# A fused alignment, attention and expert-mix kernel: the expert tiles placed two steps sooner, in the step that turns the last batch

## The reference, cut to what matters

```python
def reference(x, itok_BS_0_21, ...):
    h = _L0_tok_ref(x, itok_BS_0_21, ...)             # soft alignment, its gradient: [32, 128, 128]
    h = h + _L0_attn_ref(_layernorm(h), Wq, Wk, Wv, Wm)
    h = h + _L0_ffn_ref(_layernorm(h), Wg, W, V, W2)
    return h

def _L0_attn_ref(input1, Wq, Wk, Wv, Wm):
    ...
    A = -(Q[:, :, :, None] - K[:, :, None, :]) ** 2
    P = jax.nn.softmax(A / d ** 0.5, axis=-1)
    O = jnp.einsum('bhts,bhse->bhte', P, V)
    head_result = O.transpose(0, 2, 1, 3).reshape(B, T, E)
    return head_result @ Wm + input1

def _L0_ffn_ref(x, Wg, W, V, W2):
    topv, topi = jax.lax.top_k(jnp.einsum('bsd,de->bse', x, Wg), 2)
    ...
    for e in range(8):
        h = silu(x @ W[e]) * (x @ V[e])
        y = y + gw[..., e:e + 1] * (h @ W2[e])
```

## Time and profile before

| what | value |
|---|---|
| median of 3 runs | 694.59 us (694.49 to 696.78) |
| profiled execution, whole | 695.72 us |
| its span | 693.9 us |
| mean granted TensorE clock, share of full | 0.938 |
| PE busy | 370.7 us (53% of the span) |
| DVE busy | 496.9 us (72%) |
| ACT busy | 373.2 us (54%) |
| POOL busy | 228.7 us (33%) |

### The profile page before, as it was taken

One profiled execution on the slowest core, in us unless ns is written; L12 is line 12 of the kernel. 1 busy time (PEld: TensorE's weight loads), 2 busy tenths in 40 slices (PEclk: granted clock), 3 DMA queues, 4 the chain that ended last, 5 costly groups with the idle time before them and its releaser, 6 DMA issues.

```text
span 693.9 us, 13468 instructions
## 1 busy us (share of the span) xinstructions
PE 370.7 (53%) x3107; PEld 305.2 (44%) x3108; DVE 496.9 (72%) x1773; ACT 373.2 (54%) x1106; POOL 228.7 (33%) x430
## 2 busy tenths in 40 slices
PE   0400000000000127777767887789999999999930
PEld 0200000000000015555655665678888888888830
DVE  1969999999994578888988977876744444444425
ACT  0434444444442129998977989554455455544510
POOL 1035454545453000000004332465675333333320
PEclk9999999999999998988889979999999999999975
DMA  5177804040324332333250000122332111111129
GB/s 105 45 177 172 178 9 96 4 92 7 88 57 95 106 120 63 108 98 86 74 159 32 23 24 20 53 59 60 81 95 65 41 45 42 45 43 45 39 82 283
DMA packets 113096, 54.06 MB, mean 78 GB/s; under 512 B 56988, under 2 KB 108828, under 8 KB 112947
## 3 DMA queue, kind: packets, MB, share of 16 engines
q1 hardware_dynamic: 106478, 44.53, 26.4%
q0 software_dynamic: 4320, 8.47, 3.7%
q10 hardware_dynamic: 2237, 0.38, 0.4%
HBM read 29.61 MB, written 24.19 MB: 78 GB/s over the span
## 4 chain that ended last, share of the span: by engine, by line
DVE 34%; PE 34%; ACT 13%; issue 8%; DMA 7%; SPq 3%; ACTq 0%; DVEq 0%; POOLq 0%
PE ps L752 9%; PE ps L569 5%; DVE D L1196 5%; DVE D L1205 5%; PE ps L571 5%; PE ps L570 5%; PE ps L742 4%; DVE ps L1185 3%; ACT ps L851 3%; ACT D L857 3%; ACT sq L942 3%; DMA gb<-g_dram 3%; DVE mn L1365 2%; ACT sq L935 2%; DMA iota_sb<-in_iota 2%
## 5 line engine op out<-in xcount | busy, mean ns | idle before, releaser
L1087 POOL DMA_INDIRECT xd_dram<-pay,slot x64 | 62.2, 972 | 212.6 <-DVE pay L1444 185.4
L1108 POOL DMA_INDIRECT y_dram<-ybuf,dest x71 | 69.8, 983 | 100.1 <-DVE ybuf L1550 85.1
L1528 DVE TENSOR_TENSOR sq<-sq,ps 128x512 f32<-128x512 f32 x71 | 48.8, 688 | 70.1 <-PE ps L571 54.6
L605 PE MATMUL ps<-zdiag,ones_f 32*128 32x32 f32 x2 | 0.6, 408 | 181.3 <-DVE zdiag L1273 181.3
L1064 POOL TENSOR_TENSOR D<-D 128x128 f32<-128x128 f32 x130 | 56.2, 432 | 119.2 <-DVE D L1219 59.6
L990 ACT ACTIVATE sq<-ps 128x512 f32<-128x512 f32 x71 | 42.5, 598 | 75.7 <-PE ps L571 75.7
L857 ACT ACTIVATE D<-D 64x2 f32<-64x2 f32 (+1 forms) x154 | 31.3, 204 | 94.6 <-DVE D L1205 78.5
L605 PEld LDWEIGHTS ps<-zdiag,ones_f 32*128 32x128 f32 x2 | 0.5, 308 | 181.4 <-DVE zdiag L1273 181.4
L942 ACT ACTIVATE sq<-sq,mn 128x128 f32<-128x128 f32 x256 | 78.2, 397 | 0.0
L752 PE MATMUL ps<-wdn,xnt 128*128 x568 | 76.2, 277 | 1.9 <-issue 1.2
L752 PEld LDWEIGHTS ps<-wdn,xnt 128*128 128x128 f32 x568 | 69.0, 192 | 4.7 <-issue 4.7
(11 more groups left out here) (222 smaller groups left out, 1062.3 us busy)
## 6 DMA issues: line engine op xcount, KB each, us to landing
stage<-xd_dram SPq DMA_DIRECT2D x71, 65.0 KB
D<-th_dram SPq DMA_DIRECT2D x16, 208.0 KB, 4.0
g_dram<-D SPq DMA_DIRECT2D x14, 208.0 KB, 4.2
x_dram<-D SPq DMA_DIRECT2D x14, 208.0 KB, 4.4
h0q<-g_dram SPq DMA_DIRECT2D x8, 256.0 KB, 3.0
gb<-g_dram SPq DMA_DIRECT2D x8, 256.0 KB, 3.6
xf<-x_dram SPq DMA_DIRECT2D x8, 256.0 KB, 3.2
xb<-x_dram SPq DMA_DIRECT2D x8, 256.0 KB, 3.9
```

The costliest lines, as they stand in the source:

```text
L1087: pool.indirect_dma_start(xd_dram, bass.IndirectOffsetOnAxis(slot[:, q, j, k:k + 1], 0), pay[q % 3][:, k, j, :], None).then_inc(s_sc[2 * k ...
L1108: pool.indirect_dma_start(y_dram, bass.IndirectOffsetOnAxis(dest[:, w:w + 1], 0), yrow[w], None, bounds_check=2 * NB * T - 1, oob_is_err=F ...
```

## The change

START goes from NB + 1 to NB - 1, so tile k stands in step 31 + k. The first column and its copies move from the end of the step before the first tile to the tile's own step; on PE they stand ahead of `up(0)`. Since banks 5 and 6 are in use in step 31, `column(0)` waits for the copies of batch 31's turned scores. The wait for the copied head results (`s_num`) moves from `experts_begin` to the first `down`, since only bank 7 needs it. Nothing else is edited. The steps of the attention's pieces, of the sends, of the tables and of the first scatter keep their numbers. Because the condition in `root_second` contains START, quad 6 meets it too.

```diff
-        START, UNROLLED = NB + 1, 28
+        START, UNROLLED = NB - 1, 28
...
             def column(k, c):
 
+                if isinstance(k, int) and k < 1:
+                    pe.wait_ge(s_pta, pta(NB))
+                    pe.wait_ge(s_ptd, ptd(NB))
                 pe.wait_ge(s_xr[c], round_of(k, c))
...
             def down(k, c, e):
 
                 pe.wait_ge(s_ht, k + 1)
-                if not (isinstance(k, int) and k < 1):
+                if isinstance(k, int) and k < 1:
+                    pe.wait_ge(s_num, 2 * NQ)
+                else:
                     pe.wait_ge(s_y, k)
...
                 pe.wait_ge(s_sq, NB)
-                pe.wait_ge(s_num, 2 * NQ)
...
                 k = n - START
+                if k == 0:
+                    experts_begin()
+                    column(0, 0)
                 if k >= 0:
                     expert[k] = expert_of(k)
                     up(k, k % 4, expert[k])
...
-                if n == START - 1:
-                    experts_begin()
-                    column(0, 0)
```

More of the change, by code:

```diff
@@ L1021, in _ @@
                     weights_high(n + 1)
-                if n == START - 1:
+                k = n - START
+                if k == 0:
                     columns(0, 0)
-                k = n - START
                 if 0 <= k < UNROLLED:
```

## The result

The changed kernel takes 706.11 us (median of 6 runs, 704.14 to 709.57); the kernel before, on the same chip, takes 694.54 us (6 runs, 693.31 to 696.78). The ratio is 1.0168, with an interval of 1.0149 to 1.0187: slower by some 11.6 us. The forecast was 701.5 us, in a range of 696.7 to 705.8, and slower as the likeliest sign. So the sign came true, and the time is 0.3 us above the range and 4.6 us above the forecast. The 0.3 us are within the scatter of the runs: run again, the kernel took 10.1 us more than the one before.

A forecast was written before the change was run, and what follows sets the result against it. PE was taken to bound the tiles' stage. Start 1.3, table loads 2.8, first scatter 1.2 and clock 1.6 sum to 6.9 us over 694.6: 701.5 us, own range 698.3 to 704.9, stated range 696.7 to 705.8.

The forecast's parts named there:

- clock at the start: Half clock on PE behind the idle times at the first column and in step 32: 1.6 us together, bounds 0 and 3.2.
- What bounds the kernel: PE bounds the tiles' stage; the first tile's rows land at 447.67 wherever PE's order puts the column.
- The rival in which tiles fill the attention's waits: Rows present when PE asks, so tile work fills idle time: 690.4 us at best, chance 0.05.
- The first column: On PE at the first tile: waits 3.12 us for rows, 0.89 for copies, 0.10 ahead of `up(1)`; net 1.3 us more.
- The table loads: Two more ACT table loads in step 32 leave PE idle 2.8 us ahead of the third `up`, bounds 1.57 and 3.8.
- The rival with the page's price: ACT's table switch also pays the skill page's drain, 2.8 us dearer: 704.3 us, chance 0.04.
- The first scatter: At tile 16 DVE waits 2.9 us for scatter 0; 1.7 covered, PE idles 1.2 us, bounds 0 and 2.9.
- the clock stays down: Rival: tiles don't begin sooner and low clock lasts at the first tile, some 4 us more: 705.5 us, chance 0.16.
- From 500 us on nothing gives it back: From 500 us to the end no lost time returns, since PE stays the bound.
- the waits cover each other: Rival: start costs 1.3 us, table pair only 1.0, clock and scatter nothing: 696.9 us, chance 0.17.
- the far sum: All terms at far bounds: start 1.3, table loads 3.8, scatter 2.0, clock 3.2, together 10.3 us.
- the near sum: All terms at nearer bounds: start 1.3, table loads 1.6, scatter 0, clock 0.8, together 3.7 us.

The follow-up runs named there:

- rows of fewer quads: Changed kernel with the first table made from three quads instead of four (17 early tiles, all pads behind load 16): 704.68 us, ratio 1.0147 to the kernel before.
- the edit without the switch: Changed kernel with a plain copy for the silu of tiles 0 and 1 and no table load for quad 6: 700.84 us, ratio 1.0090 to before.
- the fill: Changed kernel plus three unread 128x512 matmuls ahead of the first column and three in step 32: 699.98 us, against the changed kernel's 705.23.

## Why the prediction was right and wrong

| term | forecast, us | after | after, run again |
|---|---|---|---|
| start and table loads (idle time of PE) | 1.3 + 2.8 | 3.5 | 3.3 |
| clock at the start | 1.6 | 3.8 | 2.4 |
| first scatter, idle time of PE | 1.2 | 2.5 | 2.0 |
| clock behind the first scatter | 0 | 2.2 | 2.0 |
| ahead of the first tile, and behind tile 21 | 0 | 1.8 | 0.1 |
| sum | 6.9 | 13.8 | 9.7 |

The idle times are read from the bracketed values: 2.71 + 0.95 + 2.65 = 6.31 us in after and 2.73 + 0.95 + 2.38 = 6.06 run again, less 0.85 + 1.06 + 0.86 = 2.77 of before. The clock's terms are what is left of the stretches, once the 0.24 us that change their side of tile 17 are put back: 7.09 + 0.24 - 3.54 and 4.90 - 0.24 - 2.49 in after.

**What bounds the kernel: right.** The first column still waits for its rows. PE came to it sooner, the load did not: issued at 446.20, it released the column at 448.26. With rows of fewer quads the wait is gone. The rival in which tiles fill the attention's waits needed the rows by 444.55 and had no ground.

**The first column: right in kind, a little too dear.** 2.71 us for 3.12, since step 31's products ended 1.0 us later in that profile and the rows landed only 0.6 us later. The copies took 0.95 us for 0.89, at half clock; at full clock, in the kernel with the rows of fewer quads, they took 0.89.

**The table loads: right.** Load, Ln, Exp, load stand between the first silus, and PE idles 2.65 us (2.38) ahead of the third `up`, where 2.8 was forecast. The silu begins at 458.63 for 455.9: later, since the half clock had stretched the products ahead, for which ACT's copy waited (454.80 for 452.0), but by the same pattern. Taking the switch out of ACT alone brings the idle time to 0.61 us. What the edit without the switch won up to tile 17 is smaller than 2.8: 1.95 us, since DVE's queue still leaves 0.61.

The rival with the page's price fell. The silu starts 1.29 us behind the start of its load of 1.28 us. The Trainium skill (ScalarE: Activation LUTs, What ACT_TABLE_LOAD costs) has a drain of 1380 ns besides. No row here shows it: from the end of the first load (456.87) to the start of the second there are 0.47 us, filled by Ln and Exp.

**The first scatter: the step that failed.** I forecast 13.84 - 10.97 = 2.9 us of waiting for DVE, of which 1.7 are covered. Piece by piece, after has:

- Gate weights to first scatter: 513.48 - 501.94 = 11.54 us. Forecast 11.54.
- Gate weights to DVE's arrival at the wait: 517.16 - 4.17 - 501.94 = 11.05 us. Forecast 10.97.
- Landing: 517.16 - 513.48 = 3.68 us. Forecast 2.3. Run again it was 3.00, with the fill 2.36.
- Cover: 4.17 - 2.49 = 1.68 us. Forecast 1.7.

So the wait was longer by the landing alone: I took the median of 71 scatters for the landing. But this wait is for the very first one, right behind eight sends. The trace of before could have told more. Scatters of its destinations between 495 and 503 us, the first three, by the view of the tile `dest`:

```profile
DMA to landing us min/median/max: 2.3/2.8/2.9
```

and in after, of the five between 511 and 519:

```profile
DMA to landing us min/median/max: 2.3/2.8/3.6
```

With 2.8 the term would have been 1.7 us, with 3.6 it is the measured 2.5. That is 1.3 us of the gap.

**No clock behind the scatter: the larger half of the same failure.** The forecast prices a fall of the clock only at the start, with both idle times there, and gave the scatter's none. I had an idle time of 1.2 us in mind, and 0.85 and 1.06 had brought no fall in before. At 1.77 and 2.49 us there was one, and it cost 2.0 and 2.2 us; at 1.61 us (silus without the table) and 1.16 us (fill) there was none. The trace of before could have told this too: the second of the two falls that the prediction named, by the transposes at 441.32, stands right behind an idle time of 1.92 us, which it did not read. Timeline and stretch of before:

```profile
439.52 1.16 PE L683 MATMUL ps<-wm_sb,ont 128*128 128x128 f32 x8 [1.92 <-DVE ont L1380]
```

```profile
440.00:444.00 4.00, 4.00 (x35) 3.62 (x37) 3.12 (x14) 0.73 (x2) 2.06 (x3) 0.57 0.16 50
```
The term's upper end, 2.9 us in the text and 2.0 in the sum, held no fall either, though its own idle time lay where a fall was to be reckoned with. Moving the scatter away shows the whole term: 3.95 us by the stretches, 4.6 by the medians, for 1.2.

**The clock at the start: mis-sized.** Forecast 1.6 us for both idle times, with bounds of 0 and 3.2. It was 2.4 us in the kernel run again, where the fill wins 2.3, and 3.8 in the result's own profile. There are two reasons. A fall cost more than 1.6 us, since more lay under it: `up(0)`, six matmuls, took 2.72 us (449.66 to 452.38) for 1.49, and each group of products some 1.0 for 0.62. And in the result's profile there were two falls, the second behind the third `up`'s 2.65 us (the stretch at 0.64; the eight matmuls at 462.44 take 1.91 us for 1.06). Run again, the 2.38 us at the same place were followed by a clock of 1.00. "The second perhaps" was right, then; the 1.6 us that I took for both were not. The rival "the clock stays down" came near in time (705.5 us), by another mechanism: the clock was back after each fall.

**From 500 us on nothing gives it back: right.** At the column of tile 21 the changed kernel is 13.0 us behind (9.3 when run again), at the end of the span 13.8 (9.7).

**The rival "the waits cover each other"** (696.9 us) fell. 696.9 is nearly what the kernel takes with both cures, 697.18 us: only with the scatter sooner and PE kept at work is the start all that is left. That the two times agree is luck: in the rival the waits were to cover each other by themselves.

**The range.** The measured 11.6 us lie above even the far sum of 10.3 us, which ends at 704.9, and above the stated 705.8. The far sum had 2.0 us for the scatter where the text's own bound was 2.9, and nothing for the clock behind it, which alone was 2.0 to 2.2 (the near sum in turn had 0.8 us for the clock where the text's bound was 0). The range also left out the upper part of the low clock, up to 707 us, and the time lay there, though by falls that ended and not by one that lasted.

## What to carry to other kernels

Before a piece is moved ahead of others, ask what releases it: if that is a transfer with its own date, the pieces that stood ahead of it were its cover, and the move turns them into idle time. Such a move also shifts everything that is numbered with it. Here the wait for the first scatter, which the kernel before did not have, and a table switch cost more than the moved piece itself. For a wait that did not exist before, take the landing of the transfers at that place, not the median of all, and price the clock with every new idle time of the size at which the trace shows falls.

## What the runs showed of the hardware

- Half clock (a granted clock of 0.50, 1.2 GHz of 2.4) followed idle times of PE of 2.71 and 2.73 us at the first column, 2.65 and, with the rows of fewer quads, 2.49 us at the third `up`, 2.49, 1.77 and, with quad 6's roots on DVE, 1.68 us at the scatter, and 1.92 us in before. It lasted 3 to 7 us, and a fall cost 1.4 to 2.4 us. Behind 1.16 and 1.61 us at the scatter, 1.60 us at quad 7's table switch, and 2.08, 2.32 and 2.38 us at the third `up` of three kernels, the clock stayed at 1.00. So the length of the idle time alone does not decide; what does besides stays open. Matmuls without use in two of the waits kept the clock at 1.00 there, and the stretch with these waits became 2.3 us shorter.
- The first indirect scatter, right behind eight sends, landed 3.68, 3.00, 2.89, 2.82 and 2.36 us after the start of its instruction in five profiles; the instruction itself takes 1.00 us of this. The median of all 71 of before is 2.3. Whether the sends ahead of it make the difference, no run shows.
- A switch of ACT's table, load, two short activations and load, takes 3.04 us from the first load to the silu (455.59 to 458.63), and the silu starts with the end of its load.
- On one chip all five kernels that ran took some 60 us longer than on the other; the one whose waits are shown had idle times of up to 16.9 us in the written-out code that the trace puts down to nothing in the core. The cause is open.
